# Four mixture-of-experts stages on one core: router bias on VectorE, second biases in one 96-row matmul, experts in pairs, four activation buffers

## The reference, cut to what matters

```python
def _ffn_ref(x, router_W, router_b, sW1, sb1, sW2, sb2, eW1, eb1, eW2, eb2):
    ...
    shared = jax.nn.relu(xt @ sW1 + sb1) @ sW2 + sb2
    logits = xt @ router_W + router_b
    probs = jax.nn.softmax(logits / T, axis=-1)
    top_p, top_i = jax.lax.top_k(probs, K)
    cw = jnp.zeros((n, E), dtype=probs.dtype)
    cw = cw.at[jnp.arange(n)[:, None], top_i].set(top_p)
    h = jax.nn.relu(jnp.einsum('nd,edh->neh', xt, eW1) + eb1)
    ye = jnp.einsum('neh,ehd->ned', h, eW2) + eb2
    routed = jnp.einsum('ned,ne->nd', ye, cw)
    return (shared + routed).reshape(b, l, d)
```

## Time and profile before

| what | us |
|---|---|
| median of 3 runs | 2795.02 (2794.58 to 2799.84) |
| profiled execution | 2787.57 |
| its span, first to last instruction | 2785.9 |
| TensorE busy in the span | 2348.0 (84%) |
| VectorE busy | 1847.1 (66%) |
| ScalarE busy | 968.7 (35%) |
| GpSimd busy | 520.9 (19%) |
| mean granted TensorE clock | 0.867 of full speed |

### The profile page before, as it was taken

One profiled execution on the slowest core, in us unless ns is written; L12 is line 12 of the kernel. 1 busy time (PEld: TensorE's weight loads), 2 busy tenths in 40 slices (PEclk: granted clock), 3 DMA queues, 4 the chain that ended last, 5 costly groups with the idle time before them and its releaser, 6 DMA issues. The chain is left out here.

```text
span 2785.9 us, 40599 instructions
## 1 busy us (share of the span) xinstructions
PE 2348.0 (84%) x13394; PEld 1757.8 (63%) x13394; DVE 1847.1 (66%) x5494; ACT 968.7 (35%) x1471; POOL 520.9 (19%) x526
## 2 busy tenths in 40 slices
PE   3777599988799987776749997889989899879999
PEld 2454488876588874545548886445555455538888
DVE  4777577753377756988767775666565665636766
ACT  1222034331133321111004333355555556543333
POOL 0000000000100002323220001343343443320000
PEclk8878699996599986666659998899999999988999
DMA  2000100000000000000000000000000000000000
GB/s 78 3 3 5 40 1 0 0 1 0 0 1 1 1 31 0 1 0 0 0 1 1 0 0 1 1 1 1 1 1 1 1 1 1 1 1 5 8 8 12
DMA packets 13840, 14.87 MB, mean 5 GB/s; under 512 B 4056, under 2 KB 11513, under 8 KB 13178
## 3 DMA queue, kind: packets, MB, share of 16 engines
q1 hardware_dynamic: 13690, 13.04, 1.5%
HBM read 10.16 MB, written 2.88 MB: 5 GB/s over the span
## 5 line engine op out<-in xcount | busy, mean ns | idle before, releaser
L2085 DVE TENSOR_REDUCE soft_mx<-psum 128x1 f32<-128x512 f32 (+3 forms) x608 | 380.7, 658 | 254.5 <-PE psum L1965 141.1
L2006 ACT ACTIVATE soft_prob<-psum 128x1024 f32<-128x1024 f32 (+3 forms) x384 | 306.2, 810 | 262.2 <-PE psum L1897 259.8
L1962 PE MATMUL psum<-soft_own,soft_stack 128*128 128x512 f32 (+3 forms) x768 | 258.3, 396 | 21.2 <-DVE soft_mx L2085 20.0
L1897 PE MATMUL psum<-soft_stack,soft_own 128*128 128x512 f32 (+3 forms) x768 | 236.4, 391 | 1.6 <-DVE soft_mx L2085 1.0
L1897 PEld LDWEIGHTS psum<-soft_stack,soft_own 128*128 128x128 f32 x768 | 120.5, 192 | 143.2 <-issue 105.4
L1912 PE MATMUL psum<-soft_prob,soft_v_pad 128*32 128x512 f32 (+3 forms) x1536 | 166.9, 506 | 42.3 <-ACT soft_o_sb L2041 31.8
L975 DVE SCALAR_TENSOR_TENSOR x<-psum,ffn1b_cw,x 128x128 f32 (+1 forms) x512 | 143.9, 344 | 67.2 <-PE psum L867 61.4
L1962 PEld LDWEIGHTS psum<-soft_own,soft_stack 128*128 128x128 f32 x768 | 150.5, 199 | 56.2 <-DVE soft_mx L2085 42.3
L975 DVE SCALAR_TENSOR_TENSOR x<-psum,ffn0b_cw,x 128x128 f32 (+1 forms) x512 | 144.2, 344 | 60.8 <-PE psum L867 50.4
L975 DVE SCALAR_TENSOR_TENSOR x<-psum,ffn1a_cw,x 128x128 f32 (+1 forms) x512 | 144.0, 344 | 58.7 <-PE psum L867 52.7
L975 DVE SCALAR_TENSOR_TENSOR x<-psum,ffn0a_cw,x 128x128 f32 (+1 forms) x512 | 144.0, 344 | 58.6 <-PE psum L867 52.7
(11 more groups left out here) (424 smaller groups left out, 4554.9 us busy)
## 6 DMA issues: line engine op xcount, KB each, us to landing
s_ffn_w<-in_ffn_w SPq DMA_DIRECT2D x4, 1024.0 KB
out_x<-x SPq DMA_DIRECT2D x8, 256.0 KB, 2.3
mamba_coef_dram<-mamba_out_coef SPq DMA_DIRECT2D x8, 96.0 KB, 1.6
s_ret_w<-in_ret_w SPq DMA_DIRECT2D x1, 640.0 KB
s_ret_cos<-in_ret_cos SPq DMA_DIRECT2D x1, 512.0 KB
s_ret_sin<-in_ret_sin SPq DMA_DIRECT2D x1, 512.0 KB
s_mamba_in<-in_mamba_in SPq DMA_DIRECT2D x1, 256.0 KB
s_soft_sel<-in_soft_sel SPq DMA_DIRECT2D x1, 256.0 KB
```

The costliest lines, as they stand in the source:

```text
L1897: ins = pe.matmul(e_ps[:, n % 2, j, low(n):BLK], own[:, u % 3, 2 * pair + j, kt * P:(kt + 1) * P], stack[:, u % HT, qb * BLK + low(n):(qb ...
L1962: ins = pe.matmul(here, stack[:, u % HT, i * P:(i + 1) * P], own[:, u % 3, g, half * BLK:half * BLK + width], start=True, stop=half != i / ...
L2006: nc.scalar.activation(prob[:, done % PROBS, :, low(n):BLK], e_ps[:, n % 2, :, low(n):BLK], ACT.Exp, scale=float(HD) ** -0.5).then_inc(exp ...
L2085: nc.vector.tensor_reduce(mx[:, i, half, heads.start:heads.stop], bank[:, 0:width * len(heads)].rearrange("p (g k) -> p g k", k=width), AX ...
```

## The change

Within a mixture stage:

- The router's bias is loaded to all 128 partitions and added by VectorE in `shift` (one more instruction, before the maximum); the four K = 1 matmuls of `route` go.
- `combine_weights` makes, from `cw`, three groups of 32 rows: a rounded part, the rest, and the rounded part again (three more VectorE instructions). `transpose_cw` transposes 96 columns in place of 16. The second biases are kept likewise as 96 rows in fp32r parts, made once per stage by one ScalarE and one VectorE instruction. In `down(15)` four 96-row fp32r matmuls come first and then the four ordinary ones, in place of alternating.
- TensorE's order becomes up(e), up(e+1), down(e-2), down(e-1) for e = 0, 2, ... 14, and at last down(14), down(15). `transpose_cw` follows down(1), `norm.transpose` follows down(3), `route` follows down(5).
- `h` has four buffers; `relu(e)` waits for `down(e-4)`. VectorE's and ScalarE's orders are as before.
- A memset of `cw_parts` (128 x 768) stands at the start of a stage, ahead of the statistics.

```diff
-                pe.wait_ge(shifted, q)
+                pe.wait_ge(logit_used, q)
                 pe.wait_ge(cwt_ready, q)
                 for j in range(GT):
-                    pe.matmul(logit_ps[:, j, 0:E], norm.xt[:, p, j * P:(j + 1) * P], w["router"][:, :],
-                              start=True, stop=False)
-                    ins = pe.matmul(logit_ps[:, j, 0:E], const["ones"][0:1, 0:P], w["router_b"][:, :],
-                                    start=False, stop=True)
+                    ins = pe.matmul(logit_ps[:, j, 0:E], norm.xt[:, p, j * P:(j + 1) * P], w["router"][:, :],
+                                    start=True, stop=True)
...
                 for j in range(GT):
                     if e == E:
-                        pe.matmul(y_ps[:, e % Y_BANKS, j, :], cwt[:, p, j * P:(j + 1) * P], w["b2"][:, :],
-                                  start=True, stop=False)
-                    ins = pe.matmul(y_ps[:, e % Y_BANKS, j, :], h[:, e % 2, j * P:(j + 1) * P], w["w2"][:, e, :],
-                                    start=(e != E), stop=True)
+                        pe.matmul(y_ps[:, e % Y_BANKS, j, :], cwt[:, p, j * P:(j + 1) * P], b2_parts[:, :],
+                                  start=(j == 0), stop=False, skip_group_check=True)
+                for j in range(GT):
+                    ins = pe.matmul(y_ps[:, e % Y_BANKS, j, :], h[:, e % H_RING, j * P:(j + 1) * P], w["w2"][:, e, :],
+                                    start=(e != E), stop=True, skip_group_check=True)
                 ins.then_inc(y_ready, 1)
 
             def body(g, p, more):
-                for e in range(NE):
-                    if e == 0:
-                        pe.wait_ge(xt_split, g + 1)
+                pe.wait_ge(xt_split, g + 1)
+                for e in range(0, NE, 2):
                     up(g, p, e)
-                    if e >= 1:
+                    up(g, p, e + 1)
+                    if e >= 2:
+                        down(g, p, e - 2)
                         down(g, p, e - 1)
-                    if more and e == 5:
+                    if e == 2:
+                        transpose_cw(g, p)
+                    if more and e == 4:
                         norm.transpose(pe, g + 1)
                     if more and e == 6:
                         route(g + 1, 1 - p)
-                    if e == 3:
-                        transpose_cw(g, p)
+                down(g, p, E - 1)
                 down(g, p, E)
...
-                chain.link(nc.vector.tensor_reduce(top[:, :], logit_ps[:, :, 0:E], AX.X, ALU.max))
-                nc.vector.tensor_tensor(prob[:, :, :], logit_ps[:, :, 0:E], wide(top[:, :], E),
+                nc.vector.tensor_tensor(prob[:, :, :], logit_ps[:, :, 0:E],
+                                        w["router_b"][:, :].unsqueeze(1).to_broadcast([P, GT, E]),
+                                        ALU.add).then_inc(logit_used, 1)
+                dve.wait_ge(logit_used, q + 1)
+                chain.link(nc.vector.tensor_reduce(top[:, :], prob[:, :, :], AX.X, ALU.max))
+                nc.vector.tensor_tensor(prob[:, :, :], prob[:, :, :], wide(top[:, :], E),
                                         ALU.subtract).then_inc(shifted, 1)
...
-                nc.vector.scalar_tensor_tensor(cw[:, p, :, 0:E], left[:, :, :], 0.0, prob[:, :, :],
-                                               ALU.is_lt, ALU.mult).then_inc(cw_ready, 1)
+                link = Chain(dve, cw_link, 2 * q).link
+                link(nc.vector.scalar_tensor_tensor(cw[:, p, :, 0:E], left[:, :, :], 0.0, prob[:, :, :],
+                                                    ALU.is_lt, ALU.mult))
+                high, low = cw_parts[:, p, :, 0:NE], cw_parts[:, p, :, 32:32 + NE]
+                link(nc.vector.tensor_copy(high.bitcast(F32R), cw[:, p, :, :]))
+                nc.vector.tensor_copy(cw_parts[:, p, :, 64:64 + NE], high)
+                nc.vector.tensor_tensor(low, cw[:, p, :, :], high, ALU.subtract).then_inc(cw_ready, 1)
 
             def add_expert(g, p, e):
-                dve.wait_ge(y_ready, NE * g + e + 2)
+                dve.wait_ge(y_ready, NE * g + e + H_RING)
```

More of the change, by code:

```diff
@@ L745 @@
 Y_BANKS = 4
+H_RING = 4
+B2_ROWS = 96
 def ffn_stage(nc, x, const, w, loaded, name, out=None, fetch=None):
@@ L764, in ffn_stage @@
         w1_parts = sb("w1_parts", [P, 2, NE, P], F32R)
-        h = sb("h", [P, 2, BLK])
+        h = sb("h", [P, H_RING, BLK])
         cw = sb("cw", [P, 2, GT, NE])
-        cwt = sb("cwt", [NE, 2, BLK])
+        cw_parts = sb("cw_parts", [P, 2, GT, B2_ROWS])
+        cwt = sb("cwt", [B2_ROWS, 2, BLK], F32R)
+        b2_parts = sb("b2_parts", [B2_ROWS, P], F32R)
         top = sb("top", [P, GT])
@@ L777, in ffn_stage @@
         cw_one, w1_high, w1_ready = sem("cw_one"), sem("w1_high"), sem("w1_ready")
+        logit_used, cw_link, b2_high, b2_ready = sem("logit_used"), sem("cw_link"), sem("b2_high"), sem("b2_ready")
         xt_high, xt_split = sem("xt_high"), sem("xt_split")
@@ L925, in _ @@
             copy_x(0, 0)
+            nc.scalar.copy(b2_parts[:, :], w["b2"][:, :]).then_inc(b2_high, 1)
             exp(0)
@@ L998, in body @@
                         combine_weights(g + 1, 1 - p)
-            nc.vector.memset(cw[:, :, :, E:NE], 1.0).then_inc(cw_one, 1)
+            nc.vector.memset(cw[:, :, :, E:NE], 1.0)
+            nc.vector.memset(cw_parts[:, :, :, :], 0.0).then_inc(cw_one, 1)
             dve.wait_ge(cw_one, 1)
-            for i, (count, start) in enumerate(((relu_done, 1), (y_ready, 1), (acc_done, Y_BANKS - 1))):
+            for i, (count, start) in enumerate(((relu_done, 1), (y_ready, H_RING - 1), (acc_done, Y_BANKS - 1))):
                 nc.vector.memset(norm.pause[:, i + 1:i + 2], 0.0).then_inc(count, start)
@@ L1012, in _ @@
             combine_weights(0, 0)
+            dve.wait_ge(b2_high, 1)
+            nc.vector.tensor_tensor(b2_parts[64:B2_ROWS, :], w["b2"][64:B2_ROWS, :], b2_parts[64:B2_ROWS, :],
+                                    ALU.subtract).then_inc(b2_ready, 1)
             blocks(dve, body)
@@ L2121, in _, with for_all @@
                 event(*ev)
+def for_all(row):
+    return row.to_broadcast([P] + list(row.shape)[1:])
 def hybrid_kernel(nc, arrays, out):
@@ L2140, in resident @@
                     shape[0] = P
-                    src = src.to_broadcast(shape)
+                    src = for_all(src)
                 homes[key] = ctx.enter_context(nc.sbuf_tensor("s_" + n, shape, src.dtype))
@@ L2176, in hybrid_kernel @@
         layer1 = ret_copies + soft_copies
-        ffn1_copies = [(dst, arrays["ffn1_" + n]) for n, (dst, _) in zip(ffn0, ffn0_copies)]
+        ffn1_copies = [(dst, for_all(arrays["ffn1_" + n]) if n in ROW_FOR_ALL else arrays["ffn1_" + n])
+                       for n, (dst, _) in zip(ffn0, ffn0_copies)]
         load_layer1 = ctx.enter_context(nc.semaphore("load_layer1"))
```

11 lines of the change are left out of this document (6 added, 5 removed).

## The result

The changed kernel takes 2836.6 us (median of 4 runs, 2823.7 to 2842.1) against 2794.8 us for the kernel before (4 runs, 2788.4 to 2799.8): a ratio of 1.0144, interval 1.0101 to 1.0187, or +41.8 us. The prediction said 2821 us in a range of 2782 to 2840. The profiled execution of after took 2823.7 us, the fastest of its four; that of before took 2787.6. This difference of 36.1 us, against the 26 forecast, is what the traces can be asked about.

What follows compares the result with a forecast made beforehand. TensorE bounded the kernel; after the change a cycle through VectorE would, at 32.6 us a block plus clock dips of 1.60. At +6.9 per stage, total +26 us: 2814 profiled, 2821 us median, range 2782 to 2840.

Steps and rivals of the forecast that it cites:

- Both waits: TensorE in each block: about 2.9 us before the transposes, for `scale`, and 1.5 before up(11), for relu(9).
- The distance with a dip: From up(0) to the next up(0): 34.2 us with a clock dip, 32.6 without; a dip in five of six blocks.
- The terms of the cycle: Block cycle: VectorE from add(8) to the transposes 20.7 us, TensorE and back to add(8) 11.9; 32.6 together.
- TensorE's savings: Per block, `route` saves 1.6 us and the biases 1.9; TensorE's own work falls from 31.63 to 28.1.
- The sum: Six block distances +9.0, first and last blocks -0.6, start -1.5: +6.9 us a stage, 27.6 for four, total +26.
- The first and last blocks: Per stage: 1.9 us less for biases, 0.9 to 1.3 more for VectorE's late start: -0.6.
- The start of a stage: At half clock, `route` loses 2.15 of 4.30 us and the memset adds 0.7: -1.5 per stage.
- code that comes late: VectorE's idle of 4.59 us behind turns of ffn1b's loop, twice; change in cost set at 0.
- rival (d): Code comes late at five to ten more turns of VectorE's loop: +23 to +46, 2844 to 2867 us; chance 0.12.
- (a): Rival: TensorE's waits come but the clock stays up: 2785 us (2779 to 2792); chance 0.13.
- (b): Rival: the clock dips in every other block, two fewer per stage: 2808 us (2798 to 2812); chance 0.14.
- (c): Rival: VectorE keeps up and TensorE alone sets the block at 28.1 us without dips: 2678 us; chance 0.06.

Runs made afterwards that it cites:

- experiment 4: Changed kernel with twelve matmuls, product never used, before the transposes to fill TensorE's wait: 2796.8 us in one run.
- Experiment 1: Changed kernel with TensorE's old unpaired order, light biases and four activation buffers kept: 2700.0 us, ratio 0.9674 to the kernel before.
- experiment 3: Changed kernel with `exp` behind relu(9) instead of relu(8) in ScalarE's order: 2790.8 us in one run.
- experiment 5: Changed kernel, pairs kept, `exp` behind relu(9) and transposes between down(4) and down(5): 2696.7 us, ratio 0.9677 to the kernel before.
- experiment 6: Changed kernel with VectorE's eight blocks as straight code instead of a loop: 2778.8 us, ratio 0.9968 to the kernel before.
- experiment 7: Changed kernel with unpaired order, and transposes, `route` and `copy_x` one expert later: 2655.9 us, ratio 0.9527 to the kernel before.
- experiment 8: Changed kernel, unpaired, transposes and `route` one expert later, VectorE's blocks as straight code: 2640.5 us, ratio 0.9476 to the kernel before.
- experiment 9: Kernel before with VectorE's blocks as straight code: 2782.4 us, ratio 0.9955.
- experiment 10: Kernel before with only the router's bias moved to VectorE, old order and two buffers: 2716.0 us, ratio 0.9718.
- experiment 12: Kernel before with router's bias on VectorE, pairs and four buffers, second biases left as they were: 2819.7 us, ratio 1.0081.
- experiment 11: Kernel before, unpaired, with only the second biases changed to 96 rows, K = 1 matmuls of `route` kept: 2763.4 us, ratio 0.9894.
- experiment 2: Kernel before with only the paired order and four activation buffers, its own biases kept: 2871.6 us, ratio 1.0277.

## Why the prediction was right, point by point

**The mechanism.** Both waits stood where they were forecast: 2.9 before the transposes was measured at 2.92, and 1.5 before up(11) at 1.12. The distance with a dip was forecast at 34.2 and measured at 34.23 to 34.35; without a dip at 32.6, which after never shows and experiment 4 shows at 32.66. Experiment 1 shows that the order is the cause, and 3 and 5 name its two places.

**The terms of the cycle.** VectorE's part from add(8) to the transposes: forecast 20.7, measured 21.05. The error is in the steps, 1.95 and not 1.88: the gap before the add is 0.19, where before had 0.12 (experiment 6). `combine_weights` and its three instructions took 0.73 (448.59 to 449.32) against 0.79. TensorE and back took 13.18 (456.20 to 469.38) with the dip in it, against 11.9 + 1.6.

**TensorE's savings.** `route` at 0.96 (forecast 0.9). The biases stand by themselves in the timeline of ffn0a's end in after:

```profile
609.66 0.64 PE L869 MATMUL psum<-ffn0a_b_parts,ffn0a_cwt 96*128 96x128 f32 x4
610.08 0.97 PEld L872 LDWEIGHTS psum<-s_ffn_w,ffn0a_h 128*128 128x128 f32 x8
610.14 1.11 PE L872 MATMUL psum<-s_ffn_w,ffn0a_h 128*128 128x128 f32 x8
```

From 609.66 to the ordinary matmuls at 610.14 it is 0.48 (forecast 0.45). The sum of 28.1 was right (experiment 7: 28.11), and that none of it would arrive was right as well.

**The sum.** Of the +36.1 between the profiled executions, the six distances from the second block to the eighth give +54.8 over four stages (from the table), where the forecast had 4 x 9.0 - 1.6 = 34.4. The 20.4 between them are: late code in ffn0a and ffn1a, four turns of 2.7 to 3.0 or 11.3; a sixth dip in each stage where five were forecast, 4 x 1.6 = 6.4; and a rest of 2.7, in part since the distances are nearer 34.3 than 34.2. The first and last blocks gave -10.3 where -2.4 was forecast: the last ended 1.4 to 1.5 earlier in each stage, as I had charged VectorE's late start to it and it caught up, and the first blocks were shorter by 0.6 to 2.2. The start of a stage:

```profile
326.68 0.70 DVE L1018 MEMSET ffn0a_cw_parts<- 128x768 f32 x1
...
337.34 1.89 PE L843 MATMUL psum<-s_ffn_router,ffn0a_n_xt 128*128 128x15 f32 x8 [0.68 <-ACT ffn0a_n_xt L188]
339.25 5.18 PE L857 MATMUL psum<-ffn0a_xt_parts,ffn0a_w_parts 128*128 128x512 f32 x12
```

The memset takes 0.70, as forecast, and `route` 1.91 where the earlier trace rows had 4.30; from VectorE's first instruction to up(0) it is 1.4 to 1.6 less in the four stages (forecast 1.5), 6.1 in all. The sum is 54.8 - 10.3 - 6.1 = 38.4; the 2.3 to 36.1 lie outside these pieces. So the profiled time missed by 10, and not by 20, since an error of 8 the other way, and 2 outside, took half of it back: that was luck. More than half of the 20 is late code.

**The step that was mis-sized** is that on the loop's turns, "code that comes late", which was set at 0 on the ground that before and after would share it. They share it in ffn1b (about 7 us in each). In ffn0b the late turns of before (33.63 and 33.57, 0.3 to 0.4 each) are gone in after (34.35 and 34.34), and in ffn0a and ffn1a after has four late turns that before has not, of about 2.8 each. Of these 2.8, 2.2 to 2.5 are the longer wait before the transposes (5.1 to 5.4 in place of 2.92), and the rest stands with the clock, whose lower level lasts longer in these blocks (0.91 in the mean, not 0.95). This is rival (d), with its place as described and a smaller size: its 4.59 was read as one pause and is two. The Trainium skill, Runtime: NRT & Kernel Launch, section Instruction fetch mechanics, says that a taken branch to code that isn't at hand stops the engine until it has been fetched, which is one reason for unrolled code. The traces agree, with a packet of code behind each long turn, and straight code has none of these pauses (experiments 6, 8 and 9).

**The median.** It lies 12.9 above the profiled execution of after, and 7.2 above in before. No trace shows why the other runs take longer. The four runs of after span 18.4 us, and the five of experiment 6, with straight code, span 3.1. But the ten of experiment 9, also with straight code, span 12.3, as much as the four of before (11.4). So late code that varies from run to run can be a part of it, and that is not shown.

**The other rivals.** (a), the clock stays up, fell: 25 dips over the four stages. Here a wait of 2.92 was followed by 1.2 GHz in every block, and a wait of 0.25 in its place in no block without late code (experiment 4). The Trainium skill, TensorE: Matmul & The Clock Gate, section Why this matters for your kernels, warns of idle gaps longer than this one. The traces show that these shorter ones can be enough. The forecast of the dips came out better than its evidence: in the earlier trace rows the lower level begins at 2600.5, 5.8 us after the transposes and behind `route`, where the blocks of before without any wait have it too (the window of 426.20 in experiment 10). Only the second late turn of ffn1b has one at its wait. And that all blocks of after have a dip was not to be had from the length of the wait, as experiment 3 shows. (b), a dip in about every other block, is what experiment 6 shows at a wait of 2.25 and experiment 3 at 2.94, not after. (c), VectorE keeps up, is what experiments 7 and 8 reach, by moving the transposes, not by VectorE getting ahead.

**What stays open.** Why before has a dip in every other block with no wait at all. It is neither its late code (experiment 9) nor full use of TensorE (experiment 8 is as full and has none). Experiment 10 keeps the K = 16 matmuls and has 2 to 4 dips a stage, with waits of at most 0.45 after the first blocks; where both kinds of narrow matmul are gone, dips are found only behind waits. By their places (experiment 10), the dips of before stand behind the K = 1 matmuls and those of experiments 10 and 12 behind the K = 16 ones. But experiment 11 keeps the K = 1 matmuls, experiment 2 keeps both kinds, and in both TensorE waits a little in each block; their blocks without late code have nearly no dip. So the narrow matmuls have to do with it where TensorE never waits, and no run shows how. Which turns of a loop come late is open as well.

## What to carry to other kernels

Before pairing or reordering a loop, follow the cycle through all engines and ask where each hand-placed piece between the steps lands: a reorder that leaves the sums alone put two pieces too early for VectorE and cost 137 us, and placing them later (experiment 5) returned all of it. Work saved on an engine that then waits is worth nothing, and by the medians here less than nothing, since the longer wait brought more dips of the clock (experiment 12). When an engine's instruction stream is on the cycle, look at its loop: the turn and the waits whose numbers are computed are costs that straight code doesn't have.

## What the runs showed of the hardware

- At some turns of VectorE's loop the next instruction came 2.7 to 3.0 us after the branch, with an 8 KB packet of kind "instruction" that starts 1.0 to 1.3 after it; at others it came after 0.25, without one. Which stages had it depended on the program, not on the code of the loop alone: the same kernel shows it in ffn0a and not in ffn0b, and the kernel before with TensorE's new order (experiment 2) shows it in all four stages, with 3.4 to 3.6 in two.
- A wait on a number worked out from the loop's register left 0.19 before each add in after and 0.12 in before, against 0.035 with a constant. Over seven adds it was 1 us of a 33 us block.
- A pause of TensorE of 2.25 was followed by a dip of the clock in 14 of 24 blocks (experiment 6), one of 2.94 in 15 of 24 (experiment 3), one of 2.92 in all 24 (after), and one of 0.65 to 0.78 in none (experiments 1, 5 and 11). A dip costs 1.6 in a block, 1.0 to 1.4 in experiment 10, and 2.9 where the lower level lasts twice as long. Twelve useless matmuls in the pause were worth 27 to 40 us (one run).
- Matmuls with K = 1 and K = 16 between those with K = 128 cost more than their own number: four K = 1 matmuls cost `route` 2.47 - 0.96 = 1.5, and the alternating K = 16 biases cost 3.15 - 0.81 = 2.3, where four fp32r matmuls of 96 rows in a row cost 0.48.
